# A graph layer with gathered rows: three tiles of 25 picked on chip, by 40 columns a turn on ScalarE and 40 or 32 on VectorE

## The chip, the cores and the metric

The kernel runs on one core of a Trainium2 chip. The metric is the device time of one execution in microseconds. In the profile the engines are PE (TensorE), ACT (ScalarE), DVE (VectorE), POOL (GpSimd) and SP (SyncE, which only issues transfers and waits). Each works through its own list of instructions in order; between lists only semaphores keep order.

## The reference

One layer of a graph network over N = 12500 nodes of 128 features and E = 400000 edges, sorted by destination.

```python
        s, d = (ei[0], ei[1])
        h = jnp.concatenate([x[s], x[d], ea], axis=-1)
        m = jax.nn.relu(h @ w1 + b1) @ w2 + b2
        agg = jax.ops.segment_sum(m, d, num_segments=x.shape[0])
        gi = agg @ w_ih + b_ih
        gh = x @ w_hh + b_hh
...
        r = jax.nn.sigmoid(i_r + h_r)
        z = jax.nn.sigmoid(i_z + h_z)
        n = jnp.tanh(i_n + r * h_n)
        return (1.0 - z) * n + z * x
    edge_index = jnp.stack([src, dst])
    h = jnp.maximum(_layernorm(x, axis=-1), 0.0)
    x = x + _L0_gnn_ref(h, edge_index, edge_attr_32, L0_gnn_w1, L0_gnn_b1, L0_gnn_w2, L0_gnn_b2, L0_gnn_w_ih, L0_gnn_b_ih, L0_gnn_w_hh, L0_gnn_b_hh)
```

## The kernel before

**Ahead of the edges** (to about 90 us) h is normalised and kept transposed on chip in `hT` (features on partitions, nodes in columns); the products h @ w1[source rows] are written to DRAM as `p_rows`.

**The edges** go in 125 chunks of G = 5 groups, a group being T = 5 tiles of 128 edges. For a group the source half of the pre-activation comes by gathers: POOL issues one indirect DMA a tile (L556), each fetching 128 rows of `p_rows` into `rows`. The destination half needs no gather: destinations are sorted, so a window of 95 nodes covers a set of groups. DVE compares (L980) to build `lhs`, PE multiplies it with the window's products (L1278), DVE adds PE's result to the gathered rows (L1015), ACT applies the ReLU (L732, L735), DVE builds a one-hot of the destinations (L971) and PE sums the messages by it (L1300); DVE adds the sums to `acc` and `deg` at the window's base (L1030, L1031).

**Picked tiles.** For some tiles the gather is replaced: the 128 columns of `hT` at the source nodes are copied, column by column, into `picked`, and PE multiplies them with `w1_keep` (L1284). Such a copy moves 4 bytes on 128 partitions at a column number held in a register. SP brings the numbers of a turn into a row on chip (L435), `load_picks` loads them into registers (L716 on ACT, L997 on DVE), and the copies follow (L724, L1005). The tiles picked are 3, 4 and, in odd chunks only, 2 (of each, the last tile of that group), that is 2.5 tiles of 25. A turn, one step of a group, picks 64 columns, half a tile: 36 on ACT with loads of 20 and 16 numbers, 28 on DVE with loads of 12, 8 and 8 (`PARTS_ACT`, `PARTS_DVE`); `TURN_TILES` says which half of which tile, and the tile is complete up to two turns before PE needs it, in odd chunks tile 4 only just.

**Order.** All lists are written by hand as steps (chunk c, group s). In step s DVE works on `lhs` of s and on sum and one-hot of s - 2, ACT on the ReLU of s - 2, PE on the pre-activation of s - 1 and the segment sums of s - 3, SP loads three groups ahead, and POOL gathers into the rows of a group once the segment sums of the chunk before have read them (`seg_ready`). The step of DVE (L1059) is: segment sums of an ended set into `acc`, then waits, then comparison, add and one-hot with a load of numbers behind each, then the 28 copies, then in s = 1, 2, 3 a part of the gates. The step of ACT (L758): `copy_q`, `copy_window` (in s = 1 and 3), `candidate`, wait, ReLU, then twice a load and its copies, then gates (s = 0) or the store of 100 finished rows (s = 4). In each chunk the gates of 100 nodes are finished: ACT issues the load of their x rows in s = 0 (L740) and the store in s = 4 (L756).

**The loop** over chunks is written out for two chunks, even and odd, and runs 60 times on every engine (L321), with chunks 0 to 3 ahead and the last one behind.

## Time and profile before

| | |
|---|---|
| median of 3 runs | 5307.78 us (5263.55 to 5307.8) |
| the profiled execution | 5254.51 us |
| its span, first to last instruction | 5252.7 us |
| mean granted clock of PE | 0.694 of full |
| DVE, ACT, PE, POOL busy | 62%, 60%, 55%, 51% |

Busy time is what an engine spent in its data instructions. Register loads, branches, waits and the issuing of transfers are not in it. Idle time before an instruction is put down to what ended it: another engine's instruction, a transfer, "remote" (a semaphore update that the records don't place) or "issue", when the engine waited for nothing that the profile shows. In a timeline successive like instructions are merged into one row with their count.

### The profile page before, as it was taken

What the parts mean: (1) busy time and instruction counts of PE and PEld (TensorE: products, weight loads), DVE (VectorE), ACT (ScalarE), POOL (GpSimd) and SP (SyncE); (2) the same over time, 40 slices, a digit from 0 to 9 for tenths busy, and PEclk for the clock granted to TensorE, in tenths of its full rate; (3) what the DMA queues carried; (4) which work ended last, traced back from release to release, by engine and by line L of the source; (5) the groups of instructions that cost most, each with busy time, mean ns of one, the idle gap of its engine ahead of it and who ended that gap; (6) DMA issues with size and microseconds to landing.
All of it is one profiled execution on the core that took longest, in us unless ns stands there. A gap on an engine that the chain in (4) does not pass through costs nothing. (4 is left out here: it accounts for less than half of the span.)

```text
span 5252.7 us, 107654 instructions
## 1 busy us (share of the span) xinstructions
PE 2875.3 (55%) x16531; PEld 2649.4 (50%) x16531; DVE 3266.3 (62%) x21990; ACT 3139.0 (60%) x24351; POOL 2688.4 (51%) x2852
## 2 busy tenths in 40 slices
PE   4555555555555555556555555555555555555555
PEld 4545545455445544545554445545445554454545
DVE  6566666566666666666666656666566666656665
ACT  5655556566556665556556556655565656556655
POOL 4555555555555554555455555545545555455554
PEclk7666767667676676666676676766676666676777
DMA  6222322233222333223233222323223322223322
GB/s 161 79 78 81 81 79 81 78 84 85 77 79 78 83 84 79 77 78 84 75 82 82 77 78 81 84 76 82 78 76 81 82 79 79 76 78 80 83 79 61
DMA packets 435834, 427.52 MB, mean 81 GB/s; under 512 B 178061, under 2 KB 329568, under 8 KB 435086
## 3 DMA queue, kind: packets, MB, share of 16 engines
q1 hardware_dynamic: 316752, 223.84, 15.0%
q0 software_dynamic: 90016, 184.53, 14.1%
q10 hardware_dynamic: 28318, 12.94, 0.9%
q14 instruction: 739, 6.05, 0.4%
q8 instruction: 9, 0.15, 0.0%
HBM read 407.93 MB, written 13.02 MB: 80 GB/s over the span
## 5 line engine op out<-in xcount | busy, mean ns | idle before, releaser
L556 POOL DMA_INDIRECT rows<-p_rows,idx x2813 | 2658.0, 945 | 2510.9 <-issue 834.9
L724 ACT COPY picked<-hT 128x4 uint8 x22464 | 2443.5, 189 | 1652.8 <-issue 1625.2
L1005 DVE COPY picked<-hT 128x4 uint8 x17472 | 1500.8, 187 | 728.4 <-issue 713.4
L1300 PE MATMUL ps<-onehot,rows 128*128 128x95 f32 x6250 | 1131.0, 345 | 749.7 <-remote 359.4
L1278 PE MATMUL ps<-rhs,lhs 128*128 128x128 f32 x6250 | 1220.4, 359 | 518.5 <-ACT rows L735 268.4
L1300 PEld LDWEIGHTS ps<-onehot,rows 128*128 128x128 f32 x6250 | 1085.0, 263 | 795.9 <-issue 794.4
L1278 PEld LDWEIGHTS ps<-rhs,lhs 128*128 128x128 f32 x6250 | 1110.7, 267 | 557.8 <-ACT rows L735 287.8
L1015 DVE TENSOR_TENSOR rows<-rows,ps 128x640 f32<-128x640 f32 x625 | 469.8, 752 | 297.4 <-issue 268.7
L980 DVE TENSOR_SCALAR_CACHE_REDUCE lhs<-dst_row,node_at 95x640 f32<-95x640 int32 x625 | 545.1, 872 | 172.3 <-issue 165.9
L732 ACT ACTIVATE rows<-rows 128x640 f32<-128x640 f32 x625 | 425.8, 681 | 214.2 <-DVE rows L1015 118.5
L971 DVE TENSOR_TENSOR onehot<-dst_rel,ps 128x475 f32<-128x475 f32 x625 | 404.1, 647 | 31.3 <-issue 24.8
L1322 PE MATMUL ps<-ident,upd 128*100 128x128 f32 x123 | 48.2, 392 | 600.9 <-DVE upd L1050 528.4
L1284 PE MATMUL ps<-w_keep,picked 128*128 128x128 f32 x624 | 162.4, 351 | 369.0 <-ACT picked L724 194.8
L1322 PEld LDWEIGHTS ps<-ident,upd 128*100 128x100 f32 x123 | 17.8, 145 | 632.4 <-DVE upd L1050 553.6
L1284 PEld LDWEIGHTS ps<-w_keep,picked 128*128 128x128 f32 x624 | 124.8, 248 | 383.9 <-issue 356.5
L1262 PE MATMUL ps<-w_dst,h_win 128*95 128x128 f32 x500 | 136.3, 367 | 97.3 <-ACT h_win L702 67.7
L1315 PE MATMUL ps<-low,b2ih 1*128 (+1 forms) x738 | 170.4, 310 | 0.0
L1030 DVE TENSOR_TENSOR acc<-acc,ps 128x95 f32 x250 | 63.6, 254 | 167.0 <-PE ps L1303 131.1
L1037 DVE SCALAR_TENSOR_TENSOR upd<-ps,bhh_col,rz 128x100 f32<-128x100 f32 x123 | 39.3, 320 | 181.5 <-remote 114.0
L1262 PEld LDWEIGHTS ps<-w_dst,h_win 128*95 128x95 f32 x500 | 94.0, 228 | 109.6 <-ACT h_win L702 71.7
L708 ACT COPY rhs<-ps 95x128 f32<-95x128 f32 x250 | 64.0, 256 | 141.2 <-issue 140.5
L1314 PE MATMUL ps<-acc,w2ih 128*128 (+1 forms) x738 | 144.6, 278 | 3.8 <-DVE out_fin L1057 3.6
(102 smaller groups left out, 1483.2 us busy)
## 6 DMA issues: line engine op xcount, KB each, us to landing
dst_row<-in_dst_rows_dram SPq DMA_DIRECT2D x625, 240.0 KB
lhs<-in_ea_t_dram SPq DMA_DIRECT2D x625, 80.0 KB
rows<-p_rows,idx POOLq DMA_INDIRECT x2813
idx<-in_src_cols_dram SPq DMA_DIRECT2D x625, 2.5 KB
low<-pick_dram SPq DMA_DIRECT2D x624, 0.2 KB
p_rows<-low SPq DMA_DIRECT2D x14, 448.0 KB, 4.5
x_fin<-in_x_dram ACTq DMA_DIRECT2D x123, 50.0 KB
out_dram<-out_fin ACTq DMA_DIRECT2D x123, 50.0 KB
```

The costliest lines, as they stand in the source:

```text
L556: pool.indirect_dma_start(out=rows[:, s, t, :], out_offset=None, in_=p_rows[:, :], in_offset=bass.IndirectOffsetOnAxis(ap=idx[:, s, t:t + ...
L724: last = nc.scalar.copy(picked_bytes[:, 4 * k:4 * k + 4], hT_bytes[:, bass.ds(place - HT_AT, 4)])
L732: nc.scalar.activation(m, m, ACT.Relu).then_inc(message_ready[s], 2 if whole else 1)
L971: nc.vector.tensor_tensor(onehot[:, ONEHOT_PLACE[s], :, 0:W], dst_rel[:, s * T:(s + 1) * T].unsqueeze(2).to_broadcast([P, T, W]), iota_ps. ...
L980: nc.vector.tensor_scalar(lhs[0:W, s, :, 0:P], dst_row[0:W, s, :].rearrange("w (t p) -> w t p", t=T), node_at[0:W, bass.ds(c * NSETS + SET ...
L1005: last = nc.vector.tensor_copy(picked_bytes[:, 4 * k:4 * k + 4], hT_bytes[:, bass.ds(place - HT_AT, 4)])
L1015: nc.vector.tensor_tensor(r, r, pre_ps[s % 2][:, 0:k * D], ALU.add).then_inc(summed[s], 1)
L1262: nc.tensor.matmul(q_ps, h_win[:], w1_dst[:], start=True, stop=True).then_inc(q_ready[k], 1)
L1278: last = nc.tensor.matmul(pre_ps[s % 2][:, t * D:(t + 1) * D], lhs[:, s, t, 0:P], rhs[:, k, :], start=True, stop=gathered)
L1284: last = nc.tensor.matmul(pre_ps[s % 2][:, t * D:(t + 1) * D], picked[:, slot * P:(slot + 1) * P], w1_keep[:], start=False, stop=True)
L1300: done = nc.tensor.matmul(sg[:, 0:W], rows[:, s, t, :], onehot[:, ONEHOT_PLACE[s], t, 0:W], start=(first and t == 0), stop=(last and t == ...
L1315: last = nc.tensor.matmul(gate_ps[:, g, :], b2ih[0:1, cols], d, start=False, stop=(g == 2))
```

## The change

Both the tiles and the turns are laid out anew, for one kind of chunk instead of an even and an odd one.

- Tiles picked: the last of groups 2, 3 and 4 in every chunk, 3 of 25, so 22 gathers a chunk. The 384 columns are cut into turns of 80, 72, 80, 72, 80, of which ACT takes 40 each, DVE 40, 32, 40, 32, 40. A turn may hold the end of one tile and the start of the next (`slots_in`). Tile 2 is complete after the second turn, tile 3 after the fourth, tile 4 after the fifth; PE multiplies them in its steps 3, 4 and 0.
- Loads of numbers: ACT 16, 16, 8; DVE 8, 12, 8, 4, 8 or 8, 12, 8, 4. The first load of a turn moves to the very start of the step, ahead of the waits; for that each step waits for the numbers of the next turn. On DVE the fifth load stands behind the second block of copies.
- The bases for `add_segments` are loaded one by one where they are used, not as a pair after step 0.
- ACT's `copy_window` goes behind the copies of its step.
- SP issues the x load and the store of finished rows, at its step 0, the store being that of the part before; ACT issues neither within the loop.
- `hT` is the first buffer, so the places in it begin at another number.
- The loop is written out for one chunk and runs 120 times. As built, its body has 243 listed instructions on ACT (before 436), 263 on DVE (413), 82 on PE (158), 25 on POOL (49).

```diff
-HALF = P // 2
-ON_CHIP = (3, 4, 2)
-NPICKS = len(ON_CHIP) * P
-TURN_TILES = (((3, 0, 0), (3, 0, 1), (4, 0, 0), (4, 0, 1), (2, 1, 0)),
-              ((2, 0, 1), (3, 0, 0), (3, 0, 1), (4, 0, 0), (4, 0, 1)))
-N_ACT, N_DVE = 36, 28
-PARTS_ACT = (20, 36)
-PARTS_DVE = (12, 20, 28)
+PICKED = (2, 3, 4)
+NPICKS = len(PICKED) * P
+N_ACT = (40, 40, 40, 40, 40)
+N_DVE = (40, 32, 40, 32, 40)
+PER_TURN = tuple(a + d for a, d in zip(N_ACT, N_DVE))
+FIRST = tuple(sum(PER_TURN[:k]) for k in range(G + 1))
+ROOM = max(PER_TURN)
+PARTS_ACT = (16, 32, 40)
+PARTS_DVE = {40: (8, 20, 28, 32, 40), 32: (8, 20, 28, 32), 24: (8, 16, 24)}
+def slots_in(turn):
+    return range(FIRST[turn] // P, (FIRST[turn + 1] - 1) // P + 1)
-HT_AT = 66688
+HT_AT = 16384 + P
...
             for c in range(first, LAG + 2):
-                body(c, c % 2)
-            with eng.Fori((LAG + 2) // 2, CHUNKS // 2) as pair:
-                for odd in range(2):
-                    body(pair * 2 + odd, odd)
-            body(CHUNKS - 1, 0)
+                body(c)
+            with eng.Fori(LAG + 2, CHUNKS - 1) as c:
+                body(c)
+            body(CHUNKS - 1)
```

SP gets the transfers of the finished rows:

```diff
+            def load_x_fin(n):
+                wait(sp, out_ready, n)
+                sp.dma_start(x_fin[:], x[bass.ds(n * FN, FN), :]).then_inc(x_fin_in, 16)
+            def store_out(n):
+                sp.wait_ge(out_ready, n + 1)
+                sp.dma_start(out[bass.ds(n * FN, FN), :], out_fin[:]).then_inc(stored, 16)
...
+                    if s == 0 and ending is not None:
+                        if not isinstance(c, int) or ending:
+                            store_out(ending - 1)
+                        load_x_fin(ending)
```

The step on ACT:

```diff
+                parts = parts_of(PARTS_ACT)
+                found = load_picks(s, parts[0])
                 if s in STARTS:
                     copy_q(c, STARTS[s])
-                starting = after(c, s, odd, 2)
-                if starting[1] in STARTS and exists(starting):
-                    copy_window(starting[0], STARTS[starting[1]])
-                if s == 0 and ending is not None:
-                    load_x_fin(ending)
                 if s == 2 and ending is not None:
                     candidate(ending)
-                old = before(c, s, odd, 2)
-                if picking(c, s):
-                    wait_picks(c, s, odd)
+                old, following = before(c, s, 2), after(c, s, 1)
+                wait_slots(c, s)
+                if exists(following):
+                    act.wait_ge(pick_in[following[1]], following[0] * 16 + 16)
                 if old:
                     relu_message(*old)
-                if picking(c, s):
-                    for part in parts_of(PARTS_ACT):
-                        pick_columns(s, odd, part, load_picks(s, part))
+                for k, part in enumerate(parts):
+                    pick_columns(s, part, found if k == 0 else load_picks(s, part))
+                starting = after(c, s, 2)
+                if starting[1] in STARTS and exists(starting):
+                    copy_window(starting[0], STARTS[starting[1]])
                 if s == 0 and ending is not None:
                     gate_activations(ending)
-                if s == 4 and ending is not None:
-                    store(ending)
```

The step on DVE:

```diff
+                parts, found = parts_of(PARTS_DVE[N_DVE[s]]), []
+                load_part()
...
+                wait_slots(c, s)
+                if exists(following):
+                    dve.wait_ge(pick_in[following[1]], following[0] * 16 + 16)
...
-                while len(found) < len(parts):
+                while len(found) < min(len(parts), 4):
                     load_part()
-                for part, places_found in zip(parts, found):
-                    pick_columns(s, odd, part, places_found)
+                for k, part in enumerate(parts):
+                    if k == 2:
+                        load_part()
+                    pick_columns(s, part, found[k])
```

What the order of the program shows. On DVE, the step s = 4 within the loop before (`low` is the row with the numbers; TENSOR_LOAD loads them):

```order
L980 TENSOR_SCALAR lhs,count<-dst_row,node_at 95x5x128 [waits pre_ready4,dst_row_in4,counted1,pre_ready2,pick_in4]
L989 TENSOR_REDUCE set_count<-count 95x1 [waits seg_ready4,lhs_ready4,lhs_ready3]
L997 TENSOR_LOAD low
L1013 ISA [waits pre_ready2]
L1015 TENSOR_TENSOR rows<-rows,ps 128x640 [waits rows_in2]
L997 TENSOR_LOAD low
L971 TENSOR_TENSOR onehot<-dst_rel,ps 128x5x95 [waits dst_rel_ready,seg_ready2]
L997 TENSOR_LOAD low
L1005 COPY picked<-hT 128x4 x28
```

and after, the same step up to its second block of 20 copies, which follows the last row:

```order
L993 TENSOR_LOAD low
L1067 ISA [waits pre_ready4]
L976 TENSOR_SCALAR lhs,count<-dst_row,node_at 95x5x128 [waits pre_ready4,counted1,dst_row_in4,pick_in0]
L985 TENSOR_REDUCE set_count<-count 95x1 [waits seg_ready4,lhs_ready4,lhs_ready3]
L993 TENSOR_LOAD low
L1008 ISA [waits pre_ready2]
L1010 TENSOR_TENSOR rows<-rows,ps 128x512 [waits rows_in2]
L993 TENSOR_LOAD low
L967 TENSOR_TENSOR onehot<-dst_rel,ps 128x5x95 [waits dst_rel_ready,seg_ready2]
L993 TENSOR_LOAD low
L1000 COPY picked<-hT 128x4 x20
L993 TENSOR_LOAD low
```

A load now stands ahead of the comparison (L976 after, L980 before) and its waits, and one between two blocks of 20 copies; the copies themselves are 40 for 28. On ACT, step s = 3 within the loop before, behind its `copy_q`:

```order
L696 ISA
L696 TENSOR_LOAD low
L702 ISA [waits q_ready1]
L702 COPY h_win<-hT 128x95
L732 ACTIVATE rows<-rows 128x640 [waits summed1,pre_ready4,pick_in3]
L716 TENSOR_LOAD low
L724 COPY picked<-hT 128x4 x20
L716 TENSOR_LOAD low
L724 COPY picked<-hT 128x4 x16
```

and after, the whole of step 3:

```order
L715 TENSOR_LOAD low
L707 COPY rhs<-ps 95x128 [waits pre_ready4,q_ready1]
L729 ACTIVATE rows<-rows 128x640 [waits pick_in4,summed1,pre_ready4,pre_ready3]
L722 COPY picked<-hT 128x4 x16
L715 TENSOR_LOAD low
L722 COPY picked<-hT 128x4 x16
L715 TENSOR_LOAD low
L722 COPY picked<-hT 128x4 x8
L695 ISA
L695 TENSOR_LOAD low
L701 ISA [waits q_ready1]
L701 COPY h_win<-hT 128x95
```

The first load has moved ahead of `copy_q` and the ReLU (L729), there are three blocks, and the window copy (L701) has moved behind them. On SP, step 0 within the loop after, behind the load of indices for group 3:

```order
L429 ISA [waits lhs_ready3]
L429 DMA dst_row<-in_dst_rows_dram 96x640
L432 DMA lhs<-in_ea_t_dram 32x5x128 [waits pre_ready3]
L283 ISA
L418 ISA [waits picked_dve,picked_act]
L418 DMA low<-pick_dram 1x72
L441 REGISTER_ALU
L442 ISA [waits out_ready]
L442 DMA out_dram<-out_fin 100x128
L438 ISA [waits out_ready]
L438 DMA x_fin<-in_x_dram 100x128
```

The store and the x load (L442, L438) stand between the numbers for one group (L418) and the indices for the next; before, neither was on this engine.

## Rows read from the trace of the kernel before

**Rows 1.** Page, part 1: busy time, share of span, instructions, by engine

```profile
PE 2875.3 (55%) x16531; PEld 2649.4 (50%) x16531; DVE 3266.3 (62%) x21990; ACT 3139.0 (60%) x24351; POOL 2688.4 (51%) x2852
```

**Rows 2.** Line L980: count, duration min/median/max, first and last start

```profile
L980 DVE TENSOR_SCALAR_CACHE_REDUCE lhs<-dst_row,node_at x625: 858/874/877, 99.3 to 5228.6; 95x640 f32<-95x640 int32 x157
```

**Rows 3.** Costliest groups, page part 5: count | busy, mean | idle before

```profile
L556 POOL DMA_INDIRECT rows<-p_rows,idx x2813 | 2658.0, 945 | 2510.9 <-issue 834.9
...
L724 ACT COPY picked<-hT 128x4 uint8 x22464 | 2443.5, 189 | 1652.8 <-issue 1625.2
...
L1005 DVE COPY picked<-hT 128x4 uint8 x17472 | 1500.8, 187 | 728.4 <-issue 713.4
```

**Rows 4.** List of waits: engine, line <- releaser: us in total, times, longest

```profile
DVE picked L1005 <- issue: 713.4, 1168, 2.4
...
POOL rows L556 <- PE ps L1303: 725.0, 126, 11.8
...
DVE cand L1040 <- remote: 154.3, 36, 5.3
...
DVE acc L1030 <- PE ps L1303: 131.1, 45, 6.9
...
ACT rows L732 <- DVE rows L1015: 118.5, 131, 3.8
...
DVE upd L1037 <- remote: 114.0, 23, 6.8
...
DVE upd L1037 <- ACT rz L747: 53.7, 31, 4.1
```

**Rows 5.** Timeline of ACT, clean: start, length, line, form, count [idle before]

```profile
2528.82 3.57 ACT L724 COPY picked<-hT 128x4 uint8 x36 [0.23 <-issue]
...
2534.66 0.67 ACT L724 COPY picked<-hT 128x4 uint8 x6 [0.76 <-issue]
```

**Rows 6.** Timeline of DVE, clean stretch

```profile
2527.96 2.09 DVE L1005 COPY picked<-hT 128x4 uint8 x28
...
2531.20 0.87 DVE L980 TENSOR_SCALAR_CACHE_REDUCE lhs<-dst_row,node_at 95x640 f32<-95x640 int32 x1
...
2532.22 0.82 DVE L1015 TENSOR_TENSOR rows<-rows,ps 128x640 f32<-128x640 f32 x1
...
2532.96 0.65 DVE L971 TENSOR_TENSOR onehot<-dst_rel,ps 128x475 f32<-128x475 f32 x1
```

**Rows 7.** Timeline of ACT, slow stretch

```profile
2546.29 0.19 ACT L724 COPY picked<-hT 128x4 uint8 x1 [0.52 <-issue]
...
2547.70 0.19 ACT L724 COPY picked<-hT 128x4 uint8 x1 [1.22 <-issue]
```

**Rows 8.** Timeline of DVE, slow stretch

```profile
2545.56 0.17 DVE L1005 COPY picked<-hT 128x4 uint8 x1 [1.18 <-issue]
```

**Rows 9.** Timeline of POOL: start of one run, both ends of another

```profile
2530.22 0.94 POOL L556 DMA_INDIRECT rows<-p_rows,idx  x1 [8.59 <-PE ps L1303]
...
2536.95 0.94 POOL L556 DMA_INDIRECT rows<-p_rows,idx  x1 [2.04 <-remote]
...
2548.19 0.95 POOL L556 DMA_INDIRECT rows<-p_rows,idx  x1 [0.30 <-issue]
```

**Rows 10.** Timeline of ACT and DVE at the jump back to the loop's start

```profile
2799.49 0.55 ACTq L756 DMA_DIRECT2D out_dram<-out_fin  x1
...
2802.72 0.26 ACT L708 COPY rhs<-ps 95x128 f32<-95x128 f32 x1 [2.18 <-issue]
...
2798.96 0.87 DVE L980 TENSOR_SCALAR_CACHE_REDUCE lhs<-dst_row,node_at 95x640 f32<-95x640 int32 x1 [1.25 <-issue]
```

**Rows 11.** Timeline of POOL and PE across their jumps back

```profile
2781.02 0.94 POOL L556 DMA_INDIRECT rows<-p_rows,idx  x1 [0.30 <-issue]
...
2792.69 0.47 PE L1317 MATMUL ps<-hT,whh_sb 128*128 x2
```

**Rows 12.** Page, part 3: DMA queue of the instructions: packets, MB, share

```profile
q14 instruction: 739, 6.05, 0.4%
```

238 lines of the change are left out of this document (108 added, 130 removed).

## The prediction

> **What bounds the kernel now.** I read the page first: VectorE (DVE) is busy 62% of the span and ScalarE (ACT) 60%, TensorE (PE) 55%, POOL 51% [rows 1]. No engine is full, so shares do not name the bound. A chunk is the unit that repeats: the comparison at L980 runs 625 times between 99.3 and 5228.6 us [rows 2], which is 8.22 us per group and 41.1 us per chunk of five groups, 125 chunks. So 1 us in a chunk is 125 us, 2.4% of the span.
>
> Then the groups of instructions. Per chunk ACT copies 180 columns and DVE 140 (22464 and 17472 in all), and POOL issues 22.5 gathers (2813) [rows 3]. The idle time before ACT's copies is 1652.8 us, of which 1625.2 is "issue": ACT waits for nobody. The list of waits says the same of DVE: 713.4 us of issue before its copies, and little for others: 131.1 us for PE's segment sums, 53.7 + 114.0 us before L1037 for ACT's gates. ACT waits 118.5 us for DVE [rows 4]. Together DVE waits for other engines about 310 us, 2.5 us a chunk (the 154.3 us before L1040 are for its own L1037, the instruction ahead), ACT 1 us. Hence these two engines' own streams set the pace together, each within 1 to 2.5 us a chunk of the other.
>
> Third, the order of time shows what "issue" is made of. In a clean stretch 36 ACT copies take 3.57 us and 28 DVE copies 2.09 us [rows 5, 6], so a copy each 97 and 71 ns: (3.57 - 0.19)/35 and (2.09 - 0.17)/27, with the length of the last copy taken off. From about 2542 to 2551 us both engines start single copies 0.71 us apart or a multiple of it [rows 7, 8]. POOL meanwhile goes on at one gather each 1.25 us: a run of ten began at 2536.95 us and the last starts at 2548.19 [rows 9]. The slow stretch starts some 4 us into that run and ends 2 us after it. A run of four gathers from 2530.22 has none: the clean turn at 2531.20 lies over it. I therefore take it that the slow stretch follows long runs of gathers, and that it costs engines time by the clock, not by their number of instructions.
>
> **The change part by part, for a chunk.**
>
> *DVE's copies.* 140 become 184 (40, 32, 40, 32, 40). 44 x 71 ns = **+3.1 us**. I know of nothing that hides them: they are on one of the two streams that set the pace.
>
> *Loads of numbers into registers, DVE.* Before there are 3 in a turn (12, 8, 8 numbers), each behind the comparison, the sum and the one-hot; these last 0.87, 0.82 and 0.65 us and the gaps between their starts (1.02 and 0.74 us) are hardly longer [rows 6], so the loads are under them. After there are 5 (8, 12, 8, 4, 8) or 4 (8, 12, 8, 4), and the order of the program shows the new first one ahead of everything in the turn. It is covered only by copies that are still queued. A load of 8 fits beside 0.65 us of one-hot, so it costs between 0 and 0.65 us a turn, 0 to 3.2 in five. ACT's 36 copies pass a load of 16 without a gap [rows 5], so the queue does cover much: I take 0.25 us, **+1.25 us**. The fifth load stands in the middle of 20 + 20 copies: 0 to 0.65 us three times, I take **+0.3**. The two single-number loads for the window's base now stand ahead of the segment sums instead of one pair behind turn 0: 0 to 0.8, I take **+0.3**, nearer the lower end because a single number is an eighth of the load that fits beside the one-hot. In a slow stretch a load costs no more than the slot it stands in. The one of [rows 7, 8] is 9 of 41 us, and shorter ones follow other runs; with a share of 40% that is **-0.75** off these three.
>
> The Trainium skill ("Advanced Engine Details and Errata", Engine Queue Depths) gives both engines a queue of 8. By it the cover would be 8 x 71 ns = 0.57 us and the first load would cost 0.1 us a turn, an estimate that makes the sum 0.8 us lower.
>
> *The jump back.* The loop body is now one chunk, so there is a jump each chunk instead of each second. At it ACT idles 2.18 us before L708 and DVE 1.25 us before L980 [rows 10], where DVE's turn at 2531.20 begins with none [rows 6] and others with up to half a microsecond. That is 1.1 us a chunk on ACT and 0.5 on DVE. PE jumps at about 2792.4 us and POOL at about 2779.8 without a gap of that kind [rows 11]. The bodies that pay are 436 (ACT) and 413 (DVE) listed instructions long, the ones of PE, 158, and POOL, 49, do not; the new ones are 243 and 263. They are nearer to PE's, so I take the jump as free: **-0.5 us** on DVE, -1.1 on ACT. The other end is +0.5 and +1.1: two jumps where there was one.
>
> The instruction queue moved 6.05 MB in 739 packets [rows 12]: far more than the program is long, so the loops of some engines are fetched again in each round.
>
> The Trainium skill ("Runtime: NRT & Kernel Launch", Instruction fetch mechanics) gives such an engine room for 512 instructions, a purely sequential prefetch, and a DMA fetch when a taken branch leaves the window. By its size alone ACT's present body of 436 would fit and yet it pays; read as a prefetch that pushes the start of the loop out, the page would have the new bodies pay too, and the sum would be that of rival 2.
>
> *ACT.* Copies 180 to 200: 20 x 97 ns = +1.9. Its first load moves ahead of the wait and the ReLU; the gap between ReLU and first copy, 0.76 us at 2534.66 [rows 5], goes, and a smaller one ahead of the wait comes: -0.35 a turn, 60% of it effective, -1.0. Three loads (16, 16, 8) for two: the third comes while copies are still queued, 0 to +0.6 a turn, I take 0. The x and out transfers leave its queue: the store takes 0.55 us to issue [rows 10], the load less, both partly under queued copies, -0.4. With the jump: **-0.6 us** (with the other end of the jump +1.6).
>
> *SP.* Two transfers more per chunk, with two waits on out_ready, ahead of the loads for groups 4 and later. Their DVE step (L1057) is over when SP comes there, since SP has just waited for that turn's copies. What is queued behind is idx and with it POOL, which waits for others anyway. 0, at worst 1 us of a later gather.
>
> *POOL.* 22.5 gathers become 22; each is 1.25 us of run. Where it shortens a long run: **-0.5 us**.
>
> *PE.* The column copies of tiles 3 and 4 now end with the turn just ahead of the product that needs them (before: every other chunk, one tile), and ACT's window copy goes behind its picks. So the segment sums behind them come later, and DVE's L1030, which waited 131.1 us, waits more: 0 to 1, I take **+0.3**.
>
> *Sum.* DVE: 3.1 + 1.25 + 0.3 + 0.3 - 0.75 - 0.5 = +3.7. Of this its 2.5 us of waiting for others swallow 2.5, since ACT gets no longer: +1.2. With -0.5 and +0.3: **+1.0 us a chunk, 125 us**. The profiled execution took 5254.5 us (span 5252.7, 1.8 around it), the median of the three runs shown is 5307.8, 1.0% above it. 5254.5 + 125 = 5380, and on the scale of the median 5380 x 1.010 = **5430 us**.
>
> **The rivals.**
>
> *1. The runs of gathers come apart: faster.* POOL's groups are released by segment sums; today it waits 725.0 us for those that end a set [rows 4] and then often gets two releases together, hence runs of 8 to 10. If PE is tied to the ends of turns (above), the releases of groups 0, 1 and 2 are a turn apart, 6 us or more, and a run of five gathers (6.25 us) is over in time. The slow stretch for a run of ten is 9 us; two of five would give perhaps 2 us each: 5 us less, at 6/7 of the copies lost in it 4.3 us. If that happens in every other chunk, -2.1 us, and the sum is -1.1 us a chunk: 5254.5 - 140, on the median's scale 5165; decided when over a quarter of the chunks lose a long run. Against it: PE's own late releases are also what bunches groups 2 and 3. Chance 0.25.
>
> *2. The jump is not free: slower still.* DVE +1.0 against the forecast (the jump at its other end, [rows 10]) and ACT at +1.6, no longer ahead: +2.3 us a chunk, 5254.5 + 288, scaled 5600. For it: both new bodies are longer than PE's, and whatever makes ACT and DVE pay today need not be length. Against: they are half as long as those that pay. Chance 0.27. This is the time that the Trainium skill's page on instruction fetch (above) gives if its sequential prefetch is taken literally.
>
> *3. ACT alone sets the pace: no change.* If DVE's waits are larger than the named ones, its +3.7 is swallowed and ACT's -0.6 and the half gather stand against PE's later sums: -0.1 us, about 5300. For it: ACT has 1.6 ms of issue, DVE half. Against: ACT's 118.5 us of waiting for DVE. Chance 0.15.
>
> The forecast, DVE over its slack with a free jump, has 0.33.
>
> **How the numbers follow.** About 1% is what a measurement of this kernel can tell from no change. Rival 1 is faster in 0.22 of its 0.25, rival 3 in 0.05, the forecast in 0.04: 0.31. Within 1%: 0.03 + 0.08 + 0.08 = 0.19. The rest, 0.50, is slower. The range goes from rival 1's time less a little to rival 2's plus the open load costs (0.5 us a chunk): 5150 to 5660. The forecast's own range is 5340 to 5530.
>
> **What would show it.** Right: DVE's first 8 to 20 copies of a turn with no more gap than now, DVE's waits before L1028 (was L1037) near zero, ACT waiting for DVE well over 118.5 us, and no 1 to 2 us of idle time at the jump. Rival 1: few runs over six gathers, issue idle before the copies well under 1600 and 700 us. Rival 2: the same 2.2 us before ACT's L707, 120 times, and as many bytes on the instruction queue. Rival 3: ACT's waits for DVE unchanged. The forecast is wrong if the loads in mid-turn open gaps at each boundary, or if slow stretches grow with the number of copies.

## The result, and the profile after

The changed kernel takes 5574.3 us (median of 4, 5550.8 to 5582.4) where the kernel before takes 5299.5 on the same chip: ratio 1.0525, 95% interval 1.0465 to 1.0585. It is slower by 275 us, 2.2 us a chunk. The forecast was 5430 us, 1.0 us a chunk over the kernel before. The two profiled executions lie 319 us apart, since that of the kernel before (5254.5) was one of its shortest. In all that follows 0.01 of ratio is 0.42 us a chunk (5299.5 / 125 / 100), and runs of different chips are compared by their ratio to the kernel before on the same chip.

Page of the changed kernel, part 1 (busy time by engine), to be read against [rows 1]; part 3 (instruction queue), against [rows 12]; and part 5 (costliest groups), against [rows 3]:

```profile
PE 3081.6 (55%) x16657; PEld 2873.6 (52%) x16657; DVE 3637.1 (65%) x27518; ACT 3321.2 (60%) x26950; POOL 2635.8 (47%) x2789
...
q14 instruction: 31, 0.25, 0.0%
...
L555 POOL DMA_INDIRECT rows<-p_rows,idx x2750 | 2605.4, 947 | 2876.9 <-PE ps L1294 1026.5
L722 ACT COPY picked<-hT 128x4 uint8 x25000 | 2634.8, 190 | 1045.6 <-issue 1036.1
L1000 DVE COPY picked<-hT 128x4 uint8 x23000 | 1892.5, 184 | 613.5 <-issue 607.7
...
L1253 PE MATMUL ps<-w_dst,h_win 128*95 128x128 f32 x500 | 181.2, 466 | 1612.4 <-ACT h_win L701 1207.3
```

VectorE is busy 370.8 us longer (3.0 us a chunk, what 44 copies at 71 ns come to), ScalarE 182 us. The idle time before the copies fell on both engines, 1625.2 to 1036.1 us and 713.4 to 607.7. The instruction queue moves 0.25 MB in place of 6.05.

List of waits of the changed kernel (us in total, times, longest), to be read against [rows 4]:

```profile
ACT rows L729 <- DVE rows L1010: 666.0, 291, 5.3
...
DVE lhs L976 <- issue: 240.4, 374, 11.8
DVE acc L1021 <- issue: 214.6, 195, 1.3
...
DVE acc L1021 <- remote: 143.3, 45, 6.0
...
DVE upd L1028 <- issue: 51.9, 94, 1.2
...
DVE acc L1021 <- PE ps L1294: 18.5, 10, 6.3
...
DVE rows L1010 <- PE ps L1275: 12.3, 24, 5.4
```

Three things stand here. ScalarE now waits 666 us for VectorE's sum, where it was 118.5: VectorE leads the pace, as forecast. VectorE has idle time at the head of its turns, put down to "issue": 240.4 us before the comparison and 214.6 before the window's sum L1021 (was L1030), where the 195 cases are 1.1 us long on average, 1.3 at most. And it still waits for others: 143.3 + 18.5 us at L1021 and 12.3 at L1010, 174 us or 1.4 us a chunk, where the forecast had all of its 2.5 us used up. All signs that the prediction named for itself came (ScalarE's long waits, nothing but "issue" before L1028, no gap of 1 to 2 us at the jump); the amount did not.

Timeline of VectorE, TensorE and POOL in the changed kernel (start, length, engine, line, operation, count, idle before):

```profile
2527.93 3.01 DVE L1000 COPY picked<-hT 128x4 uint8 x40
2536.87 0.26 DVE L1021 TENSOR_TENSOR acc<-acc,ps 128x95 f32 x1 [5.93 <-remote]
...
2538.47 0.87 DVE L976 TENSOR_SCALAR_CACHE_REDUCE lhs<-dst_row,node_at 95x640 f32<-95x640 int32 x1 [0.57 <-issue]
```

```profile
2534.01 0.25 PE L1294 MATMUL ps<-ident,set_count 95*1 95x95 f32 x1
```

```profile
2529.35 0.94 POOL L555 DMA_INDIRECT rows<-p_rows,idx  x1 [7.33 <-PE ps L1291]
...
2534.35 0.94 POOL L555 DMA_INDIRECT rows<-p_rows,idx  x1 [0.30 <-issue]
2537.42 0.94 POOL L555 DMA_INDIRECT rows<-p_rows,idx  x1 [2.12 <-remote]
```

The product that L1021 waits for ends at 2534.26, and VectorE goes on at 2536.87, 2.6 us later and 1.6 us after the end of the run of five gathers. So this "remote" wait of 5.93 us is made of 3.3 us until TensorE's product ends and 2.6 us of handover. From 400 us on there are 43 such "remote" waits. In all of them 2.6 to 3.2 us pass from the end of the product to the sum; the 10 waits that the records put down to TensorE have 0.1 to 1.6. In 22 of the 43 VectorE had been idle before the product ended, too, so that it waits 5.7 us or more; in the others it waits 0.3 to 0.5 us.

The load at the head of a turn shows differently from turn to turn. Ahead of L976 it is 0.68 us in turn 0, which is also the jump, 0.61 in turn 2 and nothing in turn 4. In turn 3 L1021 is ahead and shows 1.27 us; load_back below, without the load at the head, shows 0.62 there. The 0.57 us in the row at 2538.47 is of turn 1, behind its second load, and the kernel before has some 0.58 us at the same place.

### The profile page after: what moved, and what is told of

Read it like the earlier page. It is cut to its first block and busy times, and to the rows that moved or that the text cites. A ratio compares the mean times of both kernels' runs of the same rounds, so it can differ in the third digit from the quotient of the medians.

```text
span 5572.2 us, 119782 instructions
## 1 busy us (share of the span) xinstructions
PE 3081.6 (55%) x16657; PEld 2873.6 (52%) x16657; DVE 3637.1 (65%) x27518; ACT 3321.2 (60%) x26950; POOL 2635.8 (47%) x2789
## 5 line engine op out<-in xcount | busy, mean ns | idle before, releaser
L555 POOL DMA_INDIRECT rows<-p_rows,idx x2750 | 2605.4, 947 | 2876.9 <-PE ps L1294 1026.5
L722 ACT COPY picked<-hT 128x4 uint8 x25000 | 2634.8, 190 | 1045.6 <-issue 1036.1
L1000 DVE COPY picked<-hT 128x4 uint8 x23000 | 1892.5, 184 | 613.5 <-issue 607.7
L1269 PE MATMUL ps<-rhs,lhs 128*128 128x128 f32 x6250 | 1322.2, 389 | 11.9 <-ACT rhs L707 10.4
L1269 PEld LDWEIGHTS ps<-rhs,lhs 128*128 128x128 f32 x6250 | 1238.9, 297 | 17.5 <-ACT rhs L707 10.7
L1253 PE MATMUL ps<-w_dst,h_win 128*95 128x128 f32 x500 | 181.2, 466 | 1612.4 <-ACT h_win L701 1207.3
L729 ACT ACTIVATE rows<-rows 128x640 f32<-128x640 f32 x625 | 420.1, 672 | 1014.7 <-DVE rows L1010 666.0
L976 DVE TENSOR_SCALAR_CACHE_REDUCE lhs<-dst_row,node_at 95x640 f32<-95x640 int32 x625 | 546.9, 875 | 260.5 <-issue 239.8
L1010 DVE TENSOR_TENSOR rows<-rows,ps 128x640 f32<-128x640 f32 x625 | 462.9, 741 | 295.0 <-issue 282.3
L967 DVE TENSOR_TENSOR onehot<-dst_rel,ps 128x475 f32<-128x475 f32 x625 | 404.6, 647 | 12.3
L1021 DVE TENSOR_TENSOR acc<-acc,ps 128x95 f32 x250 | 63.5, 254 | 376.5 <-issue 214.6
L1275 PE MATMUL ps<-w_keep,picked 128*128 128x128 f32 x750 | 207.2, 373 | 9.4 <-remote 6.0
L1275 PEld LDWEIGHTS ps<-w_keep,picked 128*128 128x128 f32 x750 | 176.3, 289 | 10.0 <-issue 10.0
L957 DVE TENSOR_SCALAR dst_rel<-dst_int,base_bc 128x15 f32<-128x15 int32 x250 | 56.4, 241 | 117.7 <-issue 117.7
L1306 PEld LDWEIGHTS ps<-low,b2ih 1*128 1x128 f32 x738 | 110.4, 187 | 37.0 <-issue 2.5
```

The source lines that it names most:

```text
L555: pool.indirect_dma_start(out=rows[:, s, t, :], out_offset=None, in_=p_rows[:, :], in_offset=bass.IndirectOffsetOnAxis(ap=idx[:, s, t:t + ...
L722: last = nc.scalar.copy(picked_bytes[:, 4 * k:4 * k + 4], hT_bytes[:, bass.ds(place - HT_AT, 4)])
L729: nc.scalar.activation(m, m, ACT.Relu).then_inc(message_ready[s], 1)
L967: nc.vector.tensor_tensor(onehot[:, ONEHOT_PLACE[s], :, 0:W], dst_rel[:, s * T:(s + 1) * T].unsqueeze(2).to_broadcast([P, T, W]), iota_ps. ...
L976: nc.vector.tensor_scalar(lhs[0:W, s, :, 0:P], dst_row[0:W, s, :].rearrange("w (t p) -> w t p", t=T), node_at[0:W, bass.ds(c * NSETS + SET ...
L1000: last = nc.vector.tensor_copy(picked_bytes[:, 4 * k:4 * k + 4], hT_bytes[:, bass.ds(place - HT_AT, 4)])
```

## The experiments

**Which of the added work counts.** Four kernels derived from the changed one.

window_first:
```diff
                 if s in STARTS:
                     copy_q(c, STARTS[s])
+                starting = after(c, s, 2)
+                if starting[1] in STARTS and exists(starting):
+                    copy_window(starting[0], STARTS[starting[1]])
...
                     pick_columns(s, part, found if k == 0 else load_picks(s, part))
-                starting = after(c, s, 2)
-                if starting[1] in STARTS and exists(starting):
-                    copy_window(starting[0], STARTS[starting[1]])
```


> The changed kernel with one thing put back: ScalarE copies the window of states (copy_window) before a turn's picks and not after them. Theory (TensorE is tied to the ends of the turns: its window product waits for that copy, then the segment sums come late and VectorE waits for them at L1021, 1.7 us a chunk more than before): the waits on TensorE's window product and on L1021 shrink, and the time falls by 0.5 to 1.5 us a chunk, 60 to 190 us, to some 5380 to 5510. Rival (VectorE's own work sets the pace and its waits only change their name): within 25 us of the changed kernel, about 5575.

Measured 5646.0 us, ratio 1.0688 (1.0604 to 1.0772): slower than the changed kernel by 0.7 us a chunk, not faster. TensorE no longer waits for the window, but 1778.9 us for VectorE's update, from its page:

```profile
L1313 PE MATMUL ps<-ident,upd 128*100 128x128 f32 x123 | 55.5, 451 | 1778.9 <-DVE upd L1041 1778.9
```

TensorE's wait only changed its place. My theory fell: taking away TensorE's long waits for the window copy (1207.3 us above) gave no time back. The edit also puts the copy ahead of ScalarE's ReLU, so it does not show what those waits cost by themselves.

load_base (both kinds of VectorE's loads as before the change):
```diff
-PARTS_DVE = {40: (8, 20, 28, 32, 40), 32: (8, 20, 28, 32), 24: (8, 16, 24)}
+PARTS_DVE = {40: (12, 20, 28, 40), 32: (12, 20, 32)}
...
-                load_part()
                 done = before(c, s, AHEAD + 1)
...
-                while len(found) < min(len(parts), 4):
+                while len(found) < min(len(parts), 3):
...
-                    if k == 2:
+                    if k == 1:
...
+                    if s == 0 and not (isinstance(c, int) and c == 0):
+                        bases = load_bases(c - 1)
```


> The changed kernel with VectorE's register loads put back: no load at the head of a turn, picks loaded as 12, 8, 8 and 12 numbers behind the comparison, the sum and the one-hot, and the two base numbers loaded as a pair once a chunk. Theory (the loads at the head of the turns cost what their time is, since nothing covers them, some 0.6 us five times a chunk and twice 0.5 us for the single bases, of which placing them behind other waits gives back half): 1.0 to 2.5 us a chunk less, 125 to 310 us, to some 5260 to 5450. Rival (the price is only what the sum on record gave the loads beyond the moved one, 0.6 us): 75 us less at most, about 5500 or more; or nothing at all, where the loads stand in time that VectorE would wait in anyway.

Measured 5372.7 us, ratio 1.0176 (1.0097 to 1.0256): 1.5 us a chunk less than the changed kernel, the theory. It is the fastest kernel with three tiles that computes everything. From its list of waits:

```profile
DVE picked L1000 <- issue: 826.7, 1830, 2.3
DVE lhs L976 <- issue: 400.9, 245, 11.2
...
DVE acc L1025 <- issue: 19.6, 75, 0.5
...
DVE acc L1025 <- PE ps L1301: 4.7, 4, 2.2
...
DVE acc L1025 <- remote: 2.2, 1, 2.2
```

The idle time of issue before the window's sum (L1025, in the changed kernel L1021) is nearly gone, but it has come back before the copies and before L976. What has really gone are the waits for others: 161.8 us at the window's sum became 6.9. So the 1.5 us are not simply the length of the loads.

fewer_dve:
```diff
+LEFT = {40: {0: 6, 8: 8, 20: 6, 28: 2, 32: 6}, 32: {0: 7, 8: 10, 20: 7, 28: 4}}
...
-                for k, place in enumerate(found, FIRST[s] + N_ACT[s] + part[0]):
+                for k, place in list(enumerate(found, FIRST[s] + N_ACT[s] + part[0]))[:LEFT[N_DVE[s]].get(part[0], 40)]:
```


> The changed kernel with 44 of VectorE's 184 column copies of a chunk left out (28 a turn, as many as before the change), all register loads kept; the columns left out are zeros, so the result lacks them. Theory (VectorE sets the pace and each copy costs its 71 ns): 3.1 us a chunk less, 390 us, to some 5180. Rival (ScalarE's 40 copies a turn, or TensorE behind the turn ends, set the pace as much): less than half of that comes back, 5400 or more.

Measured 5270.2 us, ratio 0.9995 (0.9955 to 1.0035): 2.2 us a chunk less, of the 3.1 that the copies last. With the old number of copies on VectorE the rest of the change is worth nothing. From its list of waits (the profiled execution took 5341.6 us, 71 over the median):

```profile
DVE acc L1025 <- remote: 355.5, 106, 6.6
```

VectorE waits more for the window's sum than in the changed kernel (143.3 + 18.5 us). fewer_both below, the same on VectorE, has 147.8 + 260.0 us there in a profiled execution of 5325.3 us, so that it is so holds, and the split between the two names does not. This is where the missing part of the 3.1 us can be.

two_chunks:
```diff
-            with eng.Fori(LAG + 2, CHUNKS - 1) as c:
-                body(c)
+            with eng.Fori((LAG + 2) // 2, CHUNKS // 2) as pair:
+                for odd in range(2):
+                    body(pair * 2 + odd)
```


> The changed kernel with two chunks in the loop's body in place of one (60 turns of the loop for 120), nothing else. Theory (the jump back is free only because the short body stays in the engines' instruction memory; the long one has to be fetched again in each turn, as before the change, when the instruction queue moved 6.05 MB and the jump cost VectorE 1.25 us and ScalarE 2.18 us of idle time): the instruction queue moves some 6 MB or more again and the time rises by 0.5 to 1.6 us a chunk, 60 to 200 us, to 5640 to 5770. Rival (instruction fetches are hidden by other waits): the megabytes come back and the time stays within 25 us.

Measured 5533.9 us, ratio 1.0493 (1.0404 to 1.0583), not to be told from the changed kernel: the rival. From its page and VectorE's timeline, two jumps:

```profile
q14 instruction: 745, 6.10, 0.4%
```

```profile
2520.17 0.88 DVE L977 TENSOR_SCALAR_CACHE_REDUCE lhs<-dst_row,node_at 95x640 f32<-95x640 int32 x1 [3.41 <-issue]
...
2605.42 0.88 DVE L977 TENSOR_SCALAR_CACHE_REDUCE lhs<-dst_row,node_at 95x640 f32<-95x640 int32 x1 [3.29 <-issue]
```

The megabytes are back and so are 3.3 us of idle time at every second chunk, and the time does not rise. Between two jumps the body goes from one chunk to the next, and there turn 0 begins with 0 to 0.16 us of idle time:

```profile
2558.84 0.88 DVE L977 TENSOR_SCALAR_CACHE_REDUCE lhs<-dst_row,node_at 95x640 f32<-95x640 int32 x1 [0.16 <-issue]
```

So of the 0.68 us that the changed kernel has at its jump, some 0.5 are there only with a jump. VectorE's "remote" waits before the window's sum fell from 143.3 us to

```profile
DVE acc L1022 <- remote: 25.0, 42, 2.7
```

so the gap at the jump took the place of about 1 us a chunk of waits at this line.

**The loads one by one, the copies on the kernel before, and more work for ScalarE.**

base_pair:
```diff
-            def add_segments(c, k):
-                b = nc.values_load(base_i[0:1, bass.ds(c * NSETS + k, 1)], (mybir.EngineType.DVE,), min_val=0, max_val=BMAX,
+            def load_bases(c):
+                _, bases = nc.values_load_multi_w_load_instructions(
+                    base_i[0:1, bass.ds(c * NSETS, NSETS)], (mybir.EngineType.DVE,), min_val=0, max_val=BMAX,
```


> The changed kernel with only the two base numbers put back as a pair, loaded after a chunk's first turn; the load of picks at the head of each turn stays. The kernel with both loads put back took 5372.66 us, 200 us less than the changed one. Theory (each load costs its own time: a single number 0.54 us, twice a chunk, against 0.4 us once): 0.5 us a chunk less, 60 us, to some 5510. Rival (the picks' load and the base's load lie back to back ahead of VectorE's sum of a window, and that sum is what all others wait for, so the base load carries most of the 200 us): 120 us or more less.

Measured 5470.9 us, ratio 1.0380 (1.0334 to 1.0425): 0.6 us a chunk less, between the two expectations.

load_back (the edit of load_base without its last two lines):


> The changed kernel with only the loads of picks put back: 12, 8, 8 and 12 numbers behind the comparison, the sum and the one-hot, none at the head of a turn; the base numbers stay single. Theory (each load costs its own time; a load at the head of a turn is covered by nothing, one between the comparison and the sum is): 1.0 to 1.25 us a chunk less than the changed kernel, 125 to 160 us, to some 5430. Rival (the base loads carry most of the 200 us that both together gave back): within 80 us of the changed kernel, 5500 or more.

Measured 5574.4 us, ratio 1.0573 (1.0529 to 1.0618): nothing gained, by the letter the rival. But the timeline shows a second effect that I had not foreseen. Without the load at its head the loop is fetched again at each jump (page), and VectorE stands still there (timeline, two jumps):

```profile
q14 instruction: 625, 5.12, 0.3%
```

```profile
2457.42 0.88 DVE L976 TENSOR_SCALAR_CACHE_REDUCE lhs<-dst_row,node_at 95x640 f32<-95x640 int32 x1 [2.52 <-issue]
...
2501.97 0.88 DVE L976 TENSOR_SCALAR_CACHE_REDUCE lhs<-dst_row,node_at 95x640 f32<-95x640 int32 x1 [2.81 <-issue]
```

The changed kernel has 0.68 us there, so some 2 us a chunk came in as the loads went out, and load_base carries the same. What the loads at the head cost by themselves neither run can say: load_back gives nothing back, load_base 1.5 us with the bases, both with this gap in them. Why a shorter body is fetched again when a longer one is not stays open; a version of load_base whose loop stays in place wasn't tried.

before_more (on the kernel before):
```diff
+                if part[0] == 0:
+                    for k, place in enumerate(found[0:9 if s else 8]):
+                        nc.vector.tensor_copy(spare[:, (s * 9 + k) * 4:(s * 9 + k) * 4 + 4], hT_bytes[:, bass.ds(place - HT_AT, 4)])
```


> The kernel before the change with 44 more column copies a chunk on VectorE, into a spare tile that nobody reads (8 in one turn, 9 in the four others); nothing else. This prices the step of the prediction by which 2.5 us a chunk of VectorE's waits for the other engines would swallow most of what is put on it. Theory (the waits do not swallow it, since the engines waited for are themselves waiting for VectorE): 2.0 to 3.1 us a chunk more, 250 to 390 us, ratio 1.047 to 1.074. Rival (the recorded step: the waits give way): 3.1 less 2.5, under 1 us a chunk, ratio under 1.024.

Measured 5453.8 us, ratio 1.0334 (1.0274 to 1.0394), 1.4 us a chunk: under the theory, well over the rival. On the kernel before, 44 copies cost 1.4 of their 3.1 us, in the changed one 2.2. From its list of waits, to be read against [rows 3] and [rows 4]:

```profile
DVE picked L1009 <- issue: 995.2, 1541, 1.9
...
DVE acc L1034 <- PE ps L1307: 10.6, 10, 3.5
```

The wait for TensorE's sums did give way, 131.1 us to 10.6. What rose beside the copies' own time is the idle time of issue before them, 713.4 to 995.2 us.

act48 (on load_base):
```diff
-N_ACT = (40, 40, 40, 40, 40)
-N_DVE = (40, 32, 40, 32, 40)
+N_ACT = (48, 48, 48, 48, 48)
+N_DVE = (32, 24, 32, 24, 32)
```


> The kernel with both loads put back (5372.66 us) with 40 column copies a chunk moved from VectorE to ScalarE: 48 a turn on ScalarE, 32 or 24 on VectorE. Theory (VectorE sets the pace and ScalarE waits 8.7 us a chunk ahead of its rectifier, 620 us of it for VectorE's sum): VectorE loses 2.8 us a chunk and ScalarE gains 4.0 us, which its waits hold; 1 to 2.8 us a chunk less, 125 to 350 us, to some 5030 to 5250, which is below the kernel before the change. Rival (the engines are coupled turn by turn, so ScalarE's longer turns are now the pace): no gain or a loss, 5370 to 5500.

Measured 5998.4 us, ratio 1.1374 (1.1326 to 1.1421): 5.1 us a chunk slower than load_base (its loads are cut to fit) for 4.0 us of copies moved onto ScalarE and 2.8 taken off VectorE. Lists of waits:

```profile
PE ps L1260 <- ACT h_win L701: 2249.5, 228, 14.4
...
DVE acc L1025 <- remote: 386.2, 92, 6.3
DVE acc L1025 <- PE ps L1301: 384.8, 150, 8.3
...
ACT rows L729 <- DVE rows L1010: 44.2, 60, 5.5
```

ScalarE hardly waits for others any more and VectorE waits 771 us before its window's sum: ScalarE leads, and its 620 us of waits for VectorE in load_base were no room to put work into.

**ScalarE, both, fewer tiles, TensorE's picks.**

fewer_act:
```diff
-                for k, place in enumerate(found, FIRST[s] + part[0]):
+                for k, place in list(enumerate(found, FIRST[s] + part[0]))[:14]:
```


> The changed kernel with 20 of ScalarE's 200 column copies of a chunk left out (36 a turn, as many as before the change), all register loads kept; the columns left out are zeros, so the result lacks them. In the prediction ScalarE's longer turn stood at nothing, because VectorE was to set the pace. Theory (ScalarE and VectorE set it together: VectorE's sum releases ScalarE's rectifier, ScalarE's picks come before its window copy, TensorE's window sums follow from that and release VectorE's L1021): 20 copies at 99 ns are 2.0 us a chunk, and 1.0 to 2.0 us come back, 125 to 250 us, to some 5320 to 5450. Rival (the recorded step: ScalarE's copies lie beside VectorE's): within 60 us of the changed kernel, 5515 or more.

Measured 5555.0 us, ratio 1.0560 (1.0498 to 1.0623): nothing gained. The recorded step holds: ScalarE's 20 copies lie beside VectorE's.

fewer_both (the edits of fewer_dve and fewer_act):


> The changed kernel with both engines' copies cut to the number before the change (28 a turn on VectorE, 36 on ScalarE), all register loads kept; the columns left out are zeros. VectorE's cut alone gave 304 us. Theory (both are on one path around the engines): both cuts together give 400 to 550 us, to some 5030 to 5170, well below the kernel before the change, and what then remains of the change (shorter gather runs, the jump) is the gain that the added work hides. Rival (one of them hides the other): no more than 304 us together, 5270 or more.

Measured 5267.3 us, ratio 0.9998 (0.9962 to 1.0033), the same as fewer_dve: the rival. From its list of waits:

```profile
DVE acc L1025 <- PE ps L1298: 260.0, 88, 8.4
...
DVE acc L1025 <- remote: 147.8, 40, 6.6
```

two_tiles (on load_base):
```diff
-PICKED = (2, 3, 4)
-N_ACT = (40, 40, 40, 40, 40)
-N_DVE = (40, 32, 40, 32, 40)
+PICKED = (3, 4)
+N_ACT = (32, 32, 32, 32, 32)
+N_DVE = (24, 16, 24, 16, 16)
```


> The changed kernel with VectorE's loads put back (5372.66 us) and two tiles of 25 picked on chip in place of three: 32 columns a turn on ScalarE, 24 or 16 on VectorE, 23 gathers a chunk in place of 22. All of the result is computed. Theory (the two picking engines set the pace together, and gathers only through how many run back to back): ScalarE loses 40 copies at 99 ns, 4.0 us, VectorE 88 at 71 ns, 6.2 us, a chunk; one gather more is 1.25 us for GpSimd and a share of it for the others; 2.5 to 5 us a chunk less, to some 4750 to 5060, faster than both kernels. Rival (with fewer picks the gathers set the pace, 23 of them by 1.25 us in longer runs that slow all engines): 5200 to 5400, no better than the kernel before.

Measured 5641.6 us, ratio 1.0710 (1.0648 to 1.0771): 2.3 us a chunk slower than load_base with 10 us fewer copies on the two engines. Both expectations missed. List of waits:

```profile
DVE acc L1025 <- PE ps L1301: 544.4, 154, 7.5
DVE lhs L976 <- PE ps L1282: 447.8, 118, 6.1
DVE acc L1025 <- remote: 425.2, 90, 5.4
```

VectorE waits 11 us a chunk at these three, among them (L976) for TensorE's product L1282 of the picked columns. How much of it is the 23rd gather and how much the order of the slots wasn't separated.

no_pick_wait:
```diff
-                        pe.wait_ge(picked_dve, c * G + turns_of(slot))
-                        pe.wait_ge(picked_act, c * G + turns_of(slot))
-                        last = nc.tensor.matmul(pre_ps[s % 2][:, t * D:(t + 1) * D], picked[:, slot * P:(slot + 1) * P], w1_keep[:],
+                        if slot == 0:
+                            pe.wait_ge(picked_dve, c * G + turns_of(slot))
+                            pe.wait_ge(picked_act, c * G + turns_of(slot))
+                        source = ident[:] if slot else picked[:, 0:P]
+                        last = nc.tensor.matmul(pre_ps[s % 2][:, t * D:(t + 1) * D], source, w1_keep[:],
```


> The changed kernel in which TensorE multiplies a constant tile in place of the picked columns for the picked tiles 3 and 4, so that it waits for no picks there (for tile 2 it still does); all picks are still copied. The result lacks these two tiles' columns. Theory (the pace comes from VectorE's sum, ScalarE's rectifier and picks, its window copy and TensorE's sums, not from TensorE's waits for picks, which the profile shows at 0 to 9 us): within 50 us of the changed kernel. Rival (TensorE's product of picked columns just in time at the turn ends is what makes its window sums late): 100 us or more less, under 5475.

Measured 5589.3 us, ratio 1.0616 (1.0551 to 1.0680): no gain. The picks that end just ahead of TensorE's product do not set the pace.

**What gives time back.**

more_gather:
```diff
+def loaded_tiles(s):
+    return gather_tiles(s) + (1 if s == 2 else 0)
...
-                    for t in range(gather_tiles(s)):
+                    for t in range(loaded_tiles(s)):
...
-                            out=rows[:, s, t, :], out_offset=None, in_=p_rows[:, :],
+                            out=rows[:, s, t, :] if t < gather_tiles(s) else spare_rows[:, :], out_offset=None, in_=p_rows[:, :],
```


> The changed kernel with one gather more in each chunk (23 for 22), behind tile 2's four, into a spare tile that nobody reads: where the kernel before the change has its fifth gather in every second chunk. Theory (most of the 1.8 us a chunk that the change gives back comes from the gathers: half a gather less and runs of 8 and 5 in place of 9, 10 and 5): 2 to 4 us a chunk more, 250 to 500 us, to 5820 to 6070. Rival (the recorded step: half a gather is worth 0.5 us, so one is worth 1.0): 125 us more, 5700. Second rival (GpSimd has room, a gather costs nothing): 5575.

Measured 6061.7 us, ratio 1.1436 (1.1337 to 1.1536): 3.8 us a chunk for one gather, which takes POOL 1.25 us. This is the theory's amount. Its list of waits, and one handover in the timelines of VectorE, TensorE and POOL:

```profile
DVE acc L1026 <- remote: 715.8, 122, 6.1
...
DVE acc L1026 <- issue: 156.8, 126, 1.3
```

```profile
2520.60 0.25 DVE L1026 TENSOR_TENSOR acc<-acc,ps 128x95 f32 x1 [5.94 <-remote]
```

```profile
2517.45 0.25 PE L1299 MATMUL ps<-ident,set_count 95*1 95x95 f32 x1
```

```profile
2512.93 0.94 POOL L560 DMA_INDIRECT rows<-p_rows,idx  x1 [7.29 <-PE ps L1296]
...
2517.91 0.94 POOL L560 DMA_INDIRECT rows<-p_rows,idx  x1 [0.30 <-issue]
2521.15 0.94 POOL L560 DMA_INDIRECT rows<-p_rows,idx  x1 [2.30 <-remote]
```

Once in each chunk (122 times) the window's sum has such a wait, and all of them are long, 5.9 us in the mean; the changed kernel has 45, half of them short. Here 3.0 us pass until the product ends at 2517.70, and VectorE goes on at 2520.60, 2.9 us later and 1.75 us after the run of gathers has ended. The 77 cases more and their longer waits make 572 us, more than the whole rise of about 480; the rest is idle time of issue that got shorter. How the extra gather, which stands in another run, ties the window's sum to this place was not tried.

less_gather (the same loop with one gather less):
```diff
+def loaded_tiles(s):
+    return gather_tiles(s) + (-1 if s == 2 else 0)
```


> The changed kernel with one gather less in each chunk (21 for 22), the fourth of tile 2, whose rows stay what they were, so the result lacks them. Theory (the gathers and the length of their runs slow all engines): 1 to 3 us a chunk less, 125 to 375 us, to 5200 to 5450. Rival (VectorE alone sets the pace, and the gathers act only where they run long): within 60 us of the changed kernel.

Measured 5424.7 us, ratio 1.0285 (1.0201 to 1.0368): 1.0 us a chunk less, at the lower end of the theory.

act_dma:
```diff
-                    if s == 0 and ending is not None:
-                        if not isinstance(c, int) or ending:
-                            store_out(ending - 1)
-                        load_x_fin(ending)
...
+                if s == 0 and ending is not None:
+                    load_x_fin(ending)
...
+                if s == 4 and ending is not None:
+                    store(ending)
```


> The changed kernel with the loads of x and the stores of out put back on ScalarE's queue, at the places that they had before the change. Theory (ScalarE's turn has slack, since 20 of its copies count for nothing, so what it issues does not count either): within 40 us of the changed kernel, 5535 to 5615. Rival (a part of the 1.8 us a chunk that the change gives back comes from here, since ScalarE's store waits for VectorE's last sum and holds up what is behind it): 60 to 200 us more.

Measured 5718.5 us, ratio 1.0832 (1.0770 to 1.0893): 1.3 us a chunk more, the rival. By what path is not shown.

before_40_24 (on the kernel before):
```diff
-N_ACT, N_DVE = 36, 28
+N_ACT, N_DVE = 40, 24
```


> The kernel before the change with 4 columns a turn moved from VectorE to ScalarE: 40 and 24 in place of 36 and 28. Theory (VectorE sets the pace there too, and 44 copies more cost it 188 us, 4.3 us each; ScalarE has slack): 20 copies less a chunk on VectorE give 80 to 180 us back, ratio 0.966 to 0.985, faster than both kernels. Rival (ScalarE's picks hold up TensorE's product, as the profile of before shows by 262 us of waits for VectorE's sum ahead of the rectifier and 267 us of TensorE's for ScalarE's picks in the kernel with 44 more copies): the same or slower, ratio 1.00 to 1.03.

Measured 5449.2 us, ratio 1.0318 (1.0250 to 1.0386), 1.3 us a chunk more for 2.0 us onto ScalarE and 1.4 off VectorE: the rival. On the kernel before, ScalarE is as tight as VectorE. (The 262 us that this expectation reads from the profile of before are not there: ScalarE waits 118.5 us for VectorE's sum [rows 4].)

before_sp (the transfers alone on the kernel before):
```diff
+                    if s == 0 and ending is not None:
+                        if not isinstance(c, int) or ending:
+                            store_out(ending - 1)
+                        load_x_fin(ending)
...
-                if s == 0 and ending is not None:
-                    load_x_fin(ending)
...
-                if s == 4 and ending is not None:
-                    store(ending)
```


> The kernel before the change with one part of the change alone: the loads of x and the stores of out on the sync engine's queue, in the places that the change gives them there, not on ScalarE's. Theory (ScalarE's turn is as tight as VectorE's there, since moving 20 copies from VectorE to it made that kernel 168 us slower, and the transfers cost it 1.2 us a chunk as in the changed kernel): 60 to 160 us less than before, ratio 0.970 to 0.988, faster than both kernels. Rival (the gain exists only beside the new order of the picks, or VectorE holds it back): ratio 0.99 to 1.01.

Measured 5323.5 us, ratio 1.0098 (1.0062 to 1.0134): not faster but 0.4 us a chunk slower.

before_sp_window (before_sp, with the window copy behind the picks):


> The same with a second part of the change: ScalarE copies the window of states behind a turn's picks and not ahead of the rectifier. Theory (each part is a gain of its own; putting the copy back ahead cost the changed kernel about 70 us): 30 to 90 us less than with the transfers alone, ratio 0.955 to 0.98. Rival (TensorE then waits for the window, as it does 9 us a chunk in the changed kernel, and its sums come late for VectorE and GpSimd): up to 100 us more than with the transfers alone.

Measured 5328.5 us, ratio 1.0084 (1.0056 to 1.0112), the same as before_sp. Neither part is a gain on the kernel before, though putting either back costs the changed kernel 1.3 and 0.7 us a chunk. No kernel that computes all of the result was faster than the one before.

## Why the prediction was wrong

The direction was right and the amount was under half of what came: 1.0 us a chunk forecast, 2.2 measured. That the sum had the right sign with two of its terms off is in part luck. Step by step:

- **What bounds the kernel.** Right: the streams of ScalarE and VectorE together. before_more and before_40_24 show that each of them has hardly room before the change (1.4 us a chunk for 44 copies on the one, 1.3 for 20 moved to the other), and afterwards VectorE leads (fewer_dve -2.2, fewer_act nothing).
- **DVE's copies, +3.1.** Right as work (busy time +3.0); as time 2.2 in the changed kernel.
- **Of this its 2.5 us of waiting for others swallow 2.5.** This is the step that failed. VectorE's named waits went from 310 us to 174, so they took up 1.1 us a chunk, not 2.5. before_more priced the step on the kernel before, for the copies alone: by it they would have cost 0.6 us, and they cost 1.4.
- **The loads and the jump, +1.85, -0.75 and -0.5.** This is the second part of the miss. Together they stood at +0.6 us of idle time, and VectorE's idle time of issue rose by 1.4, as the table below shows.

The table sorts VectorE's time by the list of waits of each profiled execution (us; "others" is TensorE, ScalarE and "remote", at all lines):

| kernel | busy | idle, issue | idle, others |
|---|---|---|---|
| before | 3266 | 1345 | 490 |
| changed | 3637 | 1521 | 266 |
| load_base | 3657 | 1549 | 24 |
| load_back | 3674 | 1747 | 21 |
| before_more | 3680 | 1588 | 71 |
| fewer_both | 3187 | 1104 | 925 |

From before to changed this is +3.0, +1.4 and -1.8 us a chunk. The last holds the 1.1 of the named waits and 0.6 of a wait that the prediction had set aside, L1040 for VectorE's own L1037 (154.3 us to 82.1). Two things follow. The idea that waits give way is not wrong in itself: in load_base and before_more they went almost to nothing. In the changed kernel they did not, and 143.3 of the 174 us are the 45 "remote" waits before the window's sum, with their slow handover. And idle time of issue is not fixed either: it grew with the work put on VectorE (before_more, +243 us) and shrank where work was taken off (fewer_both), while the waits went the other way. My forecast let the waits shrink and held the idle time of issue to a few load costs. Why the two move against each other is not shown. A likely reason is that VectorE passes a slow stretch either with single copies, which counts as issue, or waiting for a handover. Another, also only argued, is that the engines it waits for are themselves released by VectorE's sums.

- **The loads, in parts.** The two single base numbers came to 0.6 in time (base_pair), where 0.3 stood. The load at the head of a turn shows 0.6 us of idle time in some turns and none in others, where I took 0.25 for each. The estimate by the Trainium skill ("Advanced Engine Details and Errata", Engine Queue Depths) was 0.1 us a turn; the rows of turns 2 and 3 do not bear it out, and that of turn 4 does.
- **The jump, -0.5.** Wrong: it is not free. The idle time at L976 is 0.68 us where a passage without a jump has 0 to 0.16 (two_chunks), so the jump still takes about 0.5 us a chunk of VectorE's idle time, what it took before by [rows 10] spread over two chunks. What went are the fetches: the instruction queue fell to 0.25 MB. And two_chunks, with 3.3 us of idle time at every second chunk, has the same time within the intervals, so idle time at the jump need not be time of the kernel. Rival 2 fell with it, though its 5600 us is nearer to the measured time than the forecast: its signs, 2.2 us before ScalarE's L707 and as many bytes as before, did not come. By the Trainium skill ("Runtime: NRT & Kernel Launch", Instruction fetch mechanics), read literally, the new bodies would have been fetched again in each round; the 31 packets of the changed kernel contradict that reading.
- **Slow stretches, -0.75, and half a gather, -0.5.** The first no run prices alone. For the second, one gather more costs 3.8 and one less gives 1.0, so half of one is worth 0.5 to 1.9. ScalarE's idle time of issue before its copies fell by 4.7 us a chunk.
- **The x and out transfers, -0.4 on ScalarE, counted as nothing.** Wrong: 1.3 us a chunk in the changed kernel. **ACT, 20 copies more beside VectorE's.** Right, nothing.
- **PE, later sums, +0.3.** The wait came (TensorE waits 1207.3 us for the window copy and VectorE 143.3 + 18.5 at L1021, for 131.1 + 4.0 before), its reason was another: earlier window copies made it worse and constant picks changed nothing, while one gather more made it 716 us (more_gather).
- **Rival 1**, that the runs of gathers come apart: in part. Counted over the starts in the trace, 154 runs of 8, 9 or 10 gathers became 117 of 8 or 9, none of 10. That is 37 fewer in 125 chunks, over the quarter by which it was to be decided; yet the time did not fall; VectorE's added work stood against it, and how much the shorter runs gave back was not measured alone. **Rival 3**, ScalarE alone, fell: 666 us of waits for VectorE. Its sum on record is also off: -0.6, half a gather at -0.5 and +0.3 make -0.8 us a chunk, not -0.1.

What stays open: the parts do not add up. Loads at +1.5 against transfers at -1.3, the window copy at -0.7 and half a gather at -0.5 to -1.9 would leave the rest of the change a gain of 1.0 to 2.4 us a chunk, where fewer_both shows none; and on the kernel before the transfers and the window copy are no gains at all. The order of the slots (every pick of a chunk made in the same chunk, just ahead of its use) is not tried alone, and may hold that difference.

## What to carry to other kernels

Idle time of an engine in a ring of engines that release each other is no fund to be spent at its full size. Work put on such an engine is neither free nor paid in full: 3.1 us of copies cost 1.4 us on one version of this kernel and 2.2 on another. So price it by a run that adds or leaves out the same number of copies, and look at both kinds of idle time, since one can grow as the other falls. Such a ring has also a sharp side: a gather of 1.25 us a chunk cost 3.8 us by putting the window's sum into a long wait in every chunk, so parts priced alone, or on another version of the kernel, do not add. And a small register load at the head of a turn can show as 0.6 us of idle time; taking it away is worth that only if nothing else comes in its place, as the fetch at the jump did here.

## What the chip showed that I had not expected

A handover by semaphore in the slow stretch took 2.6 to 3.2 us from the end of the product to the start of VectorE's sum (43 cases in the changed kernel). In the two shown it fell behind some four gathers in a row and was over 1.6 and 1.75 us after the run's last gather ended. Whether a loop is fetched again at its jump is no matter of its length alone: one with a load less on VectorE moved 5.12 MB and stood 2.5 to 2.8 us at each jump, where the longer body of the changed kernel moved 0.25 MB and had no gap of that kind. Two loads in a row ahead of the window's sum, of 8 numbers and of one, show as 1.1 us of idle time (214.6 us in 195 cases).
